# PE makes shifted copies and pairs of the first two chunks from the gathered rows; gram scratch laid out by blocks of eight fields

## The reference, cut to what matters

```python
e = stack([tbl_f[ids[:, f]] for f in range(64)], axis=1)      # 512 x 64 x 16
x_vec = e
for W, b in ((W0, b0), (W1, b1), (W2, b2)):                   # 128 outputs each
    z = einsum('bhd,bfd->bhfd', x_vec, e)                     # all products of a row of x_vec and a field
    x_vec = einsum('oc,bcd->bod', W, z.reshape(B, h * f, d)) + b[None, :, None]
    outs.append(x_vec.sum(axis=2))
h = concatenate([concatenate(outs, axis=1), dense_ctx], axis=1)
h = maximum(h @ W_top1 + b_top1, 0); h = maximum(h @ W_top2 + b_top2, 0)
y = h @ W_top3                                                # 512 x 1
```

## Time and profile before

| | us |
|---|---|
| median of 3 runs | 1180.73 (1180.33 to 1181.44) |
| profiled execution | 1183.49 |
| its span, first to last instruction | 1181.5 |
| around the span | 1.99 |
| PE / DVE / POOL / ACT busy in the span | 1117.9 / 997.4 / 905.2 / 681.9 |
| granted PE clock, mean of the span | 0.994 of full |

### The profile page before, as it was taken

The page is one execution under the profiler, slowest core; times in us unless marked ns, Lnnn a source line. Parts: engine busy times, 40 slices in busy tenths (PEclk is TensorE's granted clock), DMA queues, the critical chain, the costliest instruction groups (busy, mean ns, idle before and its releaser), DMA issues.

```text
span 1181.5 us, 13928 instructions
## 1 busy us (share of the span) xinstructions
PE 1117.9 (95%) x4276; PEld 745.3 (63%) x4276; DVE 997.4 (84%) x652; ACT 681.9 (58%) x695; POOL 905.2 (77%) x403
## 2 busy tenths in 40 slices
PE   0499999999999999999999999999999999999998
PEld 0256666666666666676666666666666666667685
DVE  4589899989998989899899989898998999896542
ACT  5256465665656656656656566566566665654533
POOL 6459998889988888888899888888898996575000
PEclk9999999999999999999999999999999999999999
DMA  6542424234252524252342525241523425242991
GB/s 240 170 130 65 113 74 150 65 120 121 77 155 74 157 74 140 68 152 66 109 131 71 160 74 157 74 140 64 146 76 104 136 69 160 73 152 94 294 297 46
DMA packets 103836, 142.87 MB, mean 121 GB/s; under 512 B 11745, under 2 KB 55009, under 8 KB 103042
## 3 DMA queue, kind: packets, MB, share of 16 engines
q1 hardware_dynamic: 95618, 140.42, 39.3%
q0 software_dynamic: 8192, 2.11, 2.2%
HBM read 114.96 MB, written 27.53 MB: 121 GB/s over the span
## 4 chain that ended last, share of the span: by engine, by line
PE 83%; POOL 4%; issue 3%; DMA 3%; SPq 2%; ACT 2%; DVE 1%; ACTq 0%
PE acc L1085 50%; PE acc L1079 26%; POOL z_lo L580 3%; PE turn_gram_ps L1153 3%; DMA z_float<-gram_scratch 2%; PE acc L1108 1%; POOL emb L571 1%; ACT x L878 1%; DMA z<-gram_scratch 1%; PE z_ps L1214 1%; PE turn_gram_ps L1140 1%; DMA land<-x_scratch 1%; ACT z_hi L1046 0%; DVE z_lo L816 0%; SPq L512 0%
## 5 line engine op out<-in xcount | busy, mean ns | idle before, releaser
L580 POOL TENSOR_TENSOR z_lo<-z,z_hi 128x2048 fp32r<-128x2048 f32 x143 | 659.5, 4613 | 116.8 <-ACT z_hi L849 110.3
L1085 PE MATMUL acc<-z_hi,w_hi 128*128 128x512 f32 x896 | 379.0, 423 | 6.8 <-DVE z_lo L659 4.2
L1079 PE MATMUL acc<-z_float,w_sb 128*128 128x512 f32 x768 | 349.1, 601 | 8.2 <-ACT x L878 7.6
L1085 PE MATMUL acc<-z_hi,w_lo 128*128 128x512 f32 x896 | 354.6, 396 | 0.0
L1085 PE MATMUL acc<-z_lo,w_hi 128*128 128x512 f32 x896 | 354.3, 395 | 0.0
L849 ACT ACTIVATE z_hi<-z 128x2048 fp32r<-128x2048 f32 x144 | 275.1, 1910 | 53.6 <-DVE z L647 53.6
L571 POOL DMA_INDIRECT emb<-in_tables,rows_chunk x256 | 245.4, 959 | 63.3 <-issue 51.8
L1079 PEld LDWEIGHTS acc<-z_float,w_sb 128*128 128x128 f32 x768 | 144.4, 191 | 174.6 <-issue 166.4
L858 ACT ACTIVATE z_hi<-z_ps 128x1024 fp32r<-128x1024 f32 x160 | 164.9, 1031 | 135.9 <-PE acc L1085 108.9
L659 DVE TENSOR_TENSOR z_lo<-z_ps,z_hi 128x1024 fp32r<-128x1024 f32 x160 | 194.9, 1218 | 45.3 <-ACT z_hi L858 45.3
L647 DVE TENSOR_TENSOR z<-operand_even,x_shift 128x2048 f32<-128x2048 f32 x80 | 183.0, 2287 | 37.3 <-PE acc L1085 16.6
(11 more groups left out here) (112 smaller groups left out, 640.7 us busy)
## 6 DMA issues: line engine op xcount, KB each, us to landing
land<-x_scratch SPq DMA_DIRECT2D x128, 256.0 KB
land<-x_scratch SPq DMA_DIRECT2D x128, 128.0 KB
x_shift<-x_scratch SPq DMA_DIRECT2D x16, 1024.0 KB, 5.8
gram_scratch<-gram SPq DMA_DIRECT2D x32, 512.0 KB
x_shift<-x_scratch SPq DMA_DIRECT2D x16, 768.0 KB
z_float<-gram_scratch SPq DMA_DIRECT2D x7, 1024.0 KB, 10.8
x_scratch<-emb SPq DMA_DIRECT2D x32, 192.0 KB
x_shift<-gram_scratch SPq DMA_DIRECT2D x6, 1024.0 KB, 9.2
```

The source lines that it names most:

```text
L580: pool.tensor_tensor(z_lo[:, slot], z[:, slot], z_hi[:, slot].bitcast(F32), ALU.subtract).then_inc(subtracted, 1)
L1079: mm = pe.matmul(acc[:, :], weights[:, tile0 + q, :], z_float[:, g.float_slot(pos), q, :], start=start and q == 0, stop=stop and q == QUAD ...
L1085: mm = pe.matmul(acc[:, :], w[:, tile, :], zz[:, slot, q, :], start=False, stop=stop and n == 2)
```

## The change

**Start.** Two tensors of zeros and ones are new: `turns` (128 x 2 x 160, in the tile `x2t`) and `pair_turns` (128 x 2 x 4 x 128, in the tile of `gram`, once the row numbers are computed). With one of them as weights and `emb` as the moving operand, PE writes a rotated copy of a chunk to a PSUM bank, in two matmuls of 256 columns, one for each half of the chunk (`turn`). For chunks 0 and 1 PE makes the four pairs straight in the operand banks, and the shifts 1 to 4 in `turn_gram_ps` and `x0t_ps`, from where ACT (odd) and DVE (even) copy them to `x0_shift`. The DMAs that made these are gone; shifts 5 to 7 and 0 still come by DMA. The square is taken from the bank. The last three of the 14 weight pieces are split later, in layer 1 of chunk 0, and the others use three stages. PE makes chunk 1's copies after layer 1 of chunk 0. From chunk 2 on all is as before.

**Gram scratch.** The tensor is now (row of x2, block of eight fields, half-chunk, field and sample). Of a block of 1 MB that `load_gram` reads, each partition's 8 KB lie in one piece in DRAM instead of in sixteen pieces of 512 bytes. The store, which had one piece of 4 KB for each partition, has eight of 512 bytes.

```diff
+LATE_PIECES, STAGES = 3, 3
-    gram_scratch = nc.dram_tensor("gram_scratch", (HID, 2 * CHUNKS, FIELDS, HALF_B), F32, kind="Internal").ap()
+    gram_scratch = nc.dram_tensor("gram_scratch", (HID, HALF_BLOCKS, 2 * CHUNKS, F_BLOCK * HALF_B), F32, kind="Internal").ap()
...
+        turn_banks = (turn_gram_ps[:, :], x0t_ps[:, :, :].rearrange("p b f -> p (b f)"))
...
             sp.dma_start(w_whole[:, 0:L1_SPLIT, :], w0a_split).then_inc(w0_in, 16)
+            sp.dma_start(turns_sb, turns).then_inc(turns_in, 16)
...
             sp.dma_start(w0b_stage, w0b).then_inc(w0_in, 16)
+            sp.wait_ge(rows_ready, 2)
+            sp.dma_start(pair_turns_sb, pair_turns).then_inc(turns_in, 16)
             sp.dma_start(w_whole[:, L1_SPLIT:, :], w1_split).then_inc(w1_split_in, 16)
...
             def store_gram(c, half):
...
                 sp.dma_start(bass.AP(gram_scratch.tensor, offset,
-                                     [[2 * CHUNKS * FIELDS * HALF_B, HID], [1, FIELDS * HALF_B]]),
-                             gram[:, :, :].rearrange("p f b -> p (f b)")).then_inc(gram_stored, 16)
+                                     [[2 * CHUNKS * FIELDS * HALF_B, HID], [2 * CHUNKS * F_BLOCK * HALF_B, HALF_BLOCKS],
+                                      [1, F_BLOCK * HALF_B]]),
+                             gram[:, :, :].rearrange("p (k f) b -> p k (f b)", f=F_BLOCK)).then_inc(gram_stored, 16)
...
             c0, c1 = Chunk(0, 0), Chunk(0, 1)
             store_x0(c0)
-            sp.wait_ge(x0_stored[0], 32)
-            load_pair(c0, 0)
-            load_x0(c0)
-            load_pair(c0, 1)
-            load_pair(c0, 2)
             load_x0_rest(c0)
             load_x0_base(c0)
-            load_pair(c0, 3)
             store_x0(c1)
-            load_x0(c1)
-            for m in range(PAIR_SHIFTS):
-                load_pair(c1, m)
             load_x0_rest(c1)
+            load_x0_base(c1)
             store_x1(c0)
-            load_x0_base(c1)
...
             def load_gram(k):
...
-                    gram_scratch.tensor, (half * CHUNKS * FIELDS + fb * F_BLOCK) * HALF_B,
-                    [[2 * CHUNKS * FIELDS * HALF_B, HID], [FIELDS * HALF_B, CHUNKS], [1, F_BLOCK * HALF_B]],
+                    gram_scratch.tensor, (fb * 2 + half) * CHUNKS * F_BLOCK * HALF_B,
+                    [[2 * CHUNKS * FIELDS * HALF_B, HID], [1, CHUNKS * F_BLOCK * HALF_B]],
...
+            def place_even(c):
+                for n in range(PLACED):
+                    shift = 2 * n + 2
+                    dve.wait_ge(shift_turned, c.count(QUAD, shift))
+                    dve.tensor_copy(x0_shift[:, c.par, shift, :], turn_banks[1]).then_inc(placed_even, 1)
...
             def layer1(c, pos, half=None):
...
+                if pair == 0 and (c.is_(0) or c.is_(1)):
+                    dve.wait_ge(placed_odd, c.count(PLACED, PLACED))
+                    dve.wait_ge(placed_even, c.count(PLACED, PLACED))
+                    dve.wait_ge(squared, c.count(1, 1))
...
+            place_even(c0)
             layer1(c0, 1)
             layer1(c0, 0)
...
             layer1_middle(c0)
             split_half(g0, 1)
+            for k in range(SPLIT_PIECES - LATE_PIECES, SPLIT_PIECES):
+                split_weights(k)
+            place_even(c1)
             layer1(c1, 1)
...
+            def place_odd(c):
+                for n in range(PLACED):
+                    shift = 2 * n + 1
+                    act.wait_ge(shift_turned, c.count(QUAD, shift))
+                    act.activation(x0_shift[:, c.par, shift, :], turn_banks[0], ACT.Copy).then_inc(placed_odd, 1)
+
-            to_bank(g0, 0, 0)
-            to_bank(g0, 1, 1)
             square(c0)
-            to_bank(g0, 2, 0, (formed, 1))
+            place_odd(c0)
             round_unit(g0, 1)
-            to_bank(g0, 3, 1, (formed, 2))
+            act.wait_ge(w_split, SPLIT_PIECES - LATE_PIECES)
+            act.wait_ge(placed_even, PLACED)
+            for k in range(SPLIT_PIECES - LATE_PIECES, SPLIT_PIECES):
+                act.activation(stage_of(k), piece(w_whole, k), ACT.Copy)
+                act.activation(piece(w_hi, k), piece(w_whole, k), ACT.Copy).then_inc(w_rounded, 1)
             round_half(g0, 0)
             round_half(g0, 1)
-            take_rows(c0.plus(2))
-
-            to_bank(g1, 0, 0, released_by_layer1(g0, 0))
-            to_bank(g1, 1, 1, released_by_layer1(g0, 1))
             square(c1)
+            place_odd(c1)
             act.wait_ge(const_in, 48)
-            to_bank(g1, 2, 0, (formed, g1.count(3, 1)))
             round_unit(g1, 1)
             take_x1(c0)
-            to_bank(g1, 3, 1, (formed, g1.count(3, 2)))
             round_half(g1, 0)
             round_half(g1, 1)
+            take_rows(c0.plus(2))
...
+            def turn(c, bank, weights):
+                for s in range(2):
+                    mm = pe.matmul(bank[:, s * (COLS // 2):(s + 1) * (COLS // 2)], weights(s), emb[:, c.par, :],
+                                   start=True, stop=True)
+                return mm
+            def turn_pair(c, m):
+                turn(c, operand[m % 2][:, :], lambda s: pair_turns_sb[:, s, m, :]).then_inc(copied, 1)
+            def turn_shift(c, k):
+                odd = k % 2
+                placed = placed_odd if odd else placed_even
+                if not (c.is_(0) and k <= 2):
+                    pe.wait_ge(placed, c.count(PLACED, (k - 1) // 2))
+                turn(c, turn_banks[1 - odd], lambda s: turns_sb[:, s, SHIFTS * k:SHIFTS * k + P]).then_inc(shift_turned, 1)
+            def turn_first(c):
+                g = layer1_group(c)
+                pe.wait_ge(gathered[c.par], 16 * HALF_B)
+                if not c.is_(0):
+                    pe.wait_ge(halves_formed, g.count(2))
+                turn_pair(c, 0)
+                for k in range(1, QUAD + 1):
+                    turn_shift(c, k)
+                if not c.is_(0):
+                    pe.wait_ge(formed, g.count(3))
+                turn_pair(c, 1)
+
+            def turn_rest(c):
+                g = layer1_group(c)
+                pe.wait_ge(formed, g.count(3, 1))
+                pe.wait_ge(squared, c.count(1, 1))
+                turn_pair(c, 2)
+                pe.wait_ge(formed, g.count(3, 2))
+                turn_pair(c, 3)
+
+            pe.wait_ge(turns_in, 32)
             pe.wait_ge(w0_summed, L1_PIECES + len(PLAIN_PIECES))
+            turn_first(c0)
+            turn_rest(c0)
             pe.wait_ge(w_split, L1_PIECES)
             layer1(c0)
+            pe.wait_ge(w_split, SPLIT_PIECES)
+            turn_first(c0.plus(1))
+            turn_rest(c0.plus(1))
             layer1(c0.plus(1))
```

More of the change, by code:

```diff
@@ L196, in landed @@
     def landed(self, n):
-        return self.chunk.count(LANDED * COPIES // LAND_SLOTS, LANDED * ((PAIR_SHIFTS + self.k + n) // LAND_SLOTS + 1))
+        slot = self.land_slot(n)
+        not_loaded = sum(k % LAND_SLOTS == slot for k in range(FIRST_PAIRS))
+        return self.chunk.count(LANDED * COPIES // LAND_SLOTS,
+                                LANDED * ((PAIR_SHIFTS + self.k + n) // LAND_SLOTS + 1 - not_loaded))
 def layer1_group(c):
@@ L387, in load_x0 @@
             def load_x0(c):
-                waits = [(x0_stored[c.par], c.turn(32, 32))]
-                if not (c.is_(0) or c.is_(1)):
-                    waits.append((halves_formed, Group(c.plus(-2), 4).count(2, 2)))
-                load_copies(c, 1, 5, x0_loaded, *waits)
+                load_copies(c, 1, 5, x0_loaded, (x0_stored[c.par], c.turn(32, 32)),
+                            (halves_formed, Group(c.plus(-2), 4).count(2, 2)))
             def load_x0_rest(c):
-                load_copies(c, 5, SHIFTS, x0_rest_loaded)
+                if c.is_(0) or c.is_(1):
+                    load_copies(c, 5, SHIFTS, x0_rest_loaded, (x0_stored[c.par], c.turn(32, 32)))
+                else:
+                    load_copies(c, 5, SHIFTS, x0_rest_loaded)
             def load_x0_base(c):
@@ L408, in load_pair @@
                 slot = g.land_slot(m)
-                waits = []
-                if not (c.is_(0) and m < LAND_SLOTS):
-                    waits.append((copied, g.copies(m - LAND_SLOTS + 1)))
+                waits = [(copied, g.copies(m - LAND_SLOTS + 1))]
                 if m == LAND_SLOTS:
@@ L429, in load_shift @@
                 offset, = at(c.count(X1_ROWS * COLS, i * COLS))
-                waits = [(copied, g.copies(n - LAND_SLOTS + 1))]
+                waits = []
+                if not (c.is_(0) and i < LAND_SLOTS):
+                    waits.append((copied, g.copies(n - LAND_SLOTS + 1)))
                 if i == 0:
@@ L629, in _, with split_weights @@
                 dve.tensor_tensor(w0_flat[:, cols], w0_flat[:, cols], bank, ALU.add).then_inc(w0_summed, 1)
-            for k in range(SPLIT_PIECES):
+            def split_weights(k):
                 dve.wait_ge(w_rounded, k + 1)
@@ L863, in square @@
```

(12 more changed lines are left out.)

35 lines of the change are left out of this document (25 added, 10 removed).

## The result

The changed kernel takes 1179.56 us (median of 15 runs, 1174.05 to 1179.87), the kernel before 1180.90 (15 runs, 1180.33 to 1182.90): ratio 0.9977 [0.9968, 0.9987]. That is faster by 0.23%, at the edge of what a measurement of this kernel can tell from nothing. The forecast was 1173.3, with 1170.2 to 1178.5, so the median is 6.3 us above the forecast and outside the range. The runs fall in steps that go with the mean granted clock of the execution (1.000 would be 2.4 GHz throughout): 1174.05 and 1174.44 at 0.996, 1177.6 to 1178.5 at 0.993 (four), 1179.45 to 1179.87 at 0.991 (nine). The profiled execution took 1178.15 us, its span 1176.2, at 0.993.

The account below looks back on a forecast made before the run. PE was taken as the bound, busy 1117.9 of 1181.5 us. End -7.7, start +0.3 and stores 0 took the profiled 1183.49 to 1176.1, and the median 1180.73 - 7.4 to 1173.3 us; range 1170.2 to 1178.5.

Parts of the forecast that it names:

- The end, -7.7: Gram blocks at the end: loads at 2.65 us a block, not 3.62, leave PE setting the pace, saving 7.7 us.
- Loads stay at 3.6 us: Rival for the gram loads: partitions 128 KB apart limit them, so the end gains nothing, 1181.0 us; chance 0.12.
- The stores, 0: Gram stores in the rounds: 512-byte pieces take 0.5 us more, covered by over 5 us of room; cost 0.
- Weights and first form of chunk 0: Start: layer 2 weights land at 20.3 us instead of 18.65, DVE's first form comes at 35.0 instead of 38.39.
- Layer 1 of chunk 0, 56.3 (54.8 to 57.3): Start, PE: layer 1 of chunk 0 ends at 56.3 us, before at 66.1, with 1.0 to 2.5 us for low clock.
- Chunk 1's first form, 61.5: Start: chunk 1's copies wait for chunk 0's layer 1, then take 5.2 us; DVE forms at 61.5, before at 61.50.
- Low clock in chunk 1, up to 3 us, 2.5 of it slack: Start, PE: layer 1 of chunk 1 may begin at the lower clock, up to 3 us later, 2.5 of that slack.
- Start, +0.3 (-1.5 to +3.5): Whole start, chunks 0 and 1: costs 0.3 us, between a gain of 1.5 and a loss of 3.5.
- The start loses: Rival for the start: clock and order add up, chunk 1 forms at 64, 2 to 4 us more, 1176.5; chance 0.13.
- 1180.73 - 7.4: Final sum: the profiled execution's 2.8 us over the median is carried over, so the median of 1180.73 becomes 1173.3 us.

Follow-up runs that it names:

- e1: The kernel before with only the new gram scratch layout and its matching load, all of the new start undone; 1173.84 us, ratio 0.9929.
- e12: The same kernel as e5, run again on another chip; 1191.64 us, ratio 1.0065 to the kernel before.
- e3: The changed kernel with useless matmuls on PE before the gathers land and in its pauses in chunks 0 and 1; 1173.12 us, ratio 0.9931.
- e13: The kernel before with the new gram layout alone, one later run on the chip that showed the standstill; 1174.84 us.
- e6: The changed kernel again, unedited, beside a second group of runs of the kernel before; 1177.60 us, ratio 0.9960.
- e2: The changed kernel with the old gram scratch layout, so the new start alone; 1186.25 us, ratio 1.0031 to the kernel before.
- e16: The changed kernel with 24 useless small copies each on ACT and DVE ahead of the splitting of the weights; 1174.58 us.
- e18: The same kernel as e16, one run on another chip; 1178.12 us.
- e5: The changed kernel with chunk 1's turns before chunk 0's last layer 1 unit, useless matmuls before the first rows and in chunk 0's pauses; 1170.18 us, ratio 0.9904.
- e7: The changed kernel with useless matmuls on PE only in chunk 0's two pauses; 1174.76 us, ratio 0.9943 to the kernel before.

## Why the prediction was wrong, by its own steps

- **The end, -7.7**: right. 42.1 us from the first split block to the sum (42.4 predicted), 8.2 gained there; e1 measures -8.0 by itself. Rate 411 GB/s at 1130 to 1140 us, so 2.55 us for a block, where 2.65 was taken. No gap on PE and so no clock drop.
- **Loads stay at 3.6 us** (rival, 0.12): did not happen. The distance of 128 KB between partitions, which is 128 KB in both layouts, does not hold an 8 KB piece below 411 GB/s. The distances that the prediction quotes for this rival begin at 512 KiB, so they never gave a small gain at 128 KB. That 512 bytes are enough for line rate, as the Trainium skill has it ("DMA: Bandwidth & Descriptors", Specifications), the traces do not bear out: 290 GB/s with 512 bytes, 411 with 8 KB, the same tensor.
- **The stores, 0**: right. PE's chain runs from 131.98 to the end of the last layer 2 at 1096.86, 964.88 us; before, 129.12 to 1094.04, 964.92.
- **Weights and first form of chunk 0**: right (20.78 for 20.3; 34.67 for 35.0). In the standstill executions this step fails by 16 us, or 21 in e12.
- **Layer 1 of chunk 0, 56.3 (54.8 to 57.3)**: the step that failed, by its term for the low clock. I took 3 to 6 us at the lower level for a price of 1.0 to 2.5 us, from the stretch of 0.68. But that row cuts off the low stretch of the old trace, which goes on behind it; from 54 to 64 us the same trace has
```profile
54.00:64.00 10.00, 8.47 (x16) 5.21 (x17) 5.78 (x5) 2.97 (x6) 0.00 (x0) 0.51 0.61 184
```
so some ten us at half the rate and not 3 to 6, and even 3 to 6 would cost 1.5 to 3. In the changed kernel, too, the clock was low for some ten us, from before the turn at 39.22 until 48.9, where the instructions get short again. Layer 1 ended at 58.5. With the pauses filled it ended at 53.9 (e3), so the low clock cost 4.6 us; against the 54.8 of the prediction's own count it is 3.7. "PE is continuously busy from 39.5" did not help: the clock had fallen by then.
- **Chunk 1's first form, 61.5**: 63.9, which is 58.5 + 5.4. The 5.2 for turns, last copy and handoffs was right; the lateness of layer 1 was passed on in full, as PE's queue has the turns behind it.
- **Low clock in chunk 1, up to 3 us, 2.5 of it slack**: right. It took 2.7 us (the square and the float unit take 7.4 us, 70.13 to 77.56, and 4.7 at full clock, 67.06 to 71.78), and 0.7 to 0.9 of it came through.
- **Start, +0.3 (-1.5 to +3.5)**: between the two profiled executions +2.86, of which 2.4 is chunk 1's form. That is inside the bounds. "The start loses" (0.13), with the form at 64 and 2 to 4 us, was the right case; it deserved more.
- **1180.73 - 7.4: carrying the profiled execution's 2.8 us over to the median**: the larger error, and no mechanism was given for it. By the constant 1054.37 a run of the kernel before at 1180.9 starts its chain at 126.5 and not at 129.12. The old start does vary so: e1 and e13 are the same code, chunk 1's form at 59.86 and 60.93, chain at 127.63 and 128.61, and the later one is of the kind that lacks records, as the trace of the kernel before is. So the row 61.50 was a late one, and my "before at 61.50" for a form now at 61.5 compared the new start with an unlucky old one. The new start does not have that lateness to give back: its median, 1179.56, is 1.4 above its profiled execution. Both figures are worked out from times and the constant; no trace shows a median execution of either kernel.

The miss of 6.3 us is then 2.6 (start, 2.9 for 0.3), less 0.5 (end, 8.2 for 7.7), plus 2.8 and 1.4 (each profile against its median) = 6.3. The first two parts stand in traces, the last two are such estimates. Against the median start of the kernel before, the new start costs 1179.56 - 1180.90 + 8.2 = 6.9 us in these runs and 4.2 beside e6; e2, alone, says 4.4.

## What to carry to other kernels

A layout that makes what a queue reads contiguous is worth what the rate gives until the next engine sets the pace: follow the queue to there, and the gain comes out to a few tenths (8.2 for 7.7 here). Work moved to PE at the start of a kernel inherits PE's clock and PE's order: fill PE's pauses, and put what another engine waits for ahead of the last unit, or the move gives back what it brought. And before a row of the old trace is the mark that the new start has to reach, ask whether that execution was a typical one: here it was 2.8 us over the median, and by the constant all of that lay in the rows that the change replaces. A stretch of the clock is read to its end, too: a row of ten us that cuts it makes it look short.

## What was not expected of the hardware

- The time of one kernel falls in steps of the granted clock of its execution: 1174.2, 1178 and 1179.7 us at 0.996, 0.993 and 0.991. Between the first two it is whether the clock falls in chunk 0 (e16 and e18, one code, 3.5 us); the third has no trace. With PE filled (e5) four runs lay within 0.5 us.
- Pauses of PE of 2.42 and 1.07 us with one turn of 1.13 between them were followed by the lower level (granted 0.53 from 39 to 49 us) for some 9 us of continuous work, and with the same pauses filled (e7) it was 1.00 there. In e16 it was 1.00 with the pauses as they were.
- A standstill of some 15 us on two engines, which came with one kind of start, on one chip at one time, and changes the sign of the result. A version timed on one chip only is not yet known; the layout alone (e1, e13) is the safe part.
